# A two-layer transformer kernel with routed experts: the last steps of attention 1 reordered, its last query loads issued one per step

## The reference

```
x = x + tanh(g_xattn[1]) * attention_1(layernorm(x), ctx)      # per block: 32 heads of 8, causal, 128 x 128
z = layernorm(x)                                               # per token
logits = z @ w_gate                                            # [2048, 8]
idx = argmax(softmax(logits))                                  # one of E = 8 experts for a token
loc = cumsum(onehot(idx)) - onehot(idx)                        # place in that expert's queue
keep = loc < 256                                               # capacity: 2048 / 8
h = gelu(dispatched(z) @ w1[e]);  y = h @ w2[e]                # per expert, 256 tokens, 256 -> 1024 -> 256
x = x + tanh(g_ffn[1]) * gate * y                              # back to the kept tokens
```

## Time and profile before

| | |
|---|---|
| median of 3 runs | 1349.39 us (1348.5 to 1352.16) |
| the profiled execution's own time | 1351.38 us |
| its span, first to last instruction | 1349.6 us |
| busy: TensorE, VectorE, ScalarE, POOL | 1253.2, 1092.6, 946.8, 705.6 us |
| chain that ended last | TensorE 77%, VectorE 14%, unexplained issue 3%, ScalarE 2%, DMA 2%, POOL 1% |
| TensorE's granted clock, mean | 0.98 of full speed |

### The profile page before, as it was taken

How to read it: one execution, slowest core, us unless ns; L and a number is a source line. 1 busy time by engine, 2 the same in 40 slices (tenths; PEclk the granted TensorE clock), 3 DMA queues, 4 the chain that set the end, 5 groups by cost and what they waited for, 6 DMA issues and landing times.

```text
span 1349.6 us, 28140 instructions
## 1 busy us (share of the span) xinstructions
PE 1253.2 (93%) x10492; PEld 1091.1 (81%) x10492; DVE 1092.6 (81%) x2203; ACT 946.8 (70%) x2153; POOL 705.6 (52%) x618
## 2 busy tenths in 40 slices
PE   1688999999999999999999999979999999995998
PEld 1577999999999999999999999866776454454998
DVE  8979889999989999989999999986434778765554
ACT  5799877778887778887788887645122466572775
POOL 5657555565665566655655554442000356563575
PEclk9889999999999999999999999999999999996999
DMA  4222332222123222133221010024544324217662
GB/s 146 87 62 69 99 95 87 76 71 65 54 78 88 76 69 68 52 79 89 65 70 35 26 36 24 23 68 140 64 75 72 67 42 74 60 45 242 214 231 80
DMA packets 117574, 110.05 MB, mean 82 GB/s; under 512 B 12187, under 2 KB 101499, under 8 KB 117312
## 3 DMA queue, kind: packets, MB, share of 16 engines
q1 hardware_dynamic: 114320, 99.03, 27.5%
q0 software_dynamic: 2944, 9.19, 1.9%
q10 hardware_dynamic: 176, 0.04, 0.0%
HBM read 80.20 MB, written 28.07 MB: 80 GB/s over the span
## 4 chain that ended last, share of the span: by engine, by line
PE 77%; DVE 14%; issue 3%; ACT 2%; DMA 2%; POOL 1%; POOLq 0%; SPq 0%; ACTq 0%; DVEq 0%
PE PC L577 8%; PE SS L543 7%; PE PO L559 7%; PE B L521 5%; PE PA L479 4%; PE PA L481 4%; PE B L1224 3%; PE PO L1208 2%; PE B L1734 2%; PE SS L535 2%; PE PA L492 2%; PE PA L491 2%; PE PA L493 2%; PE SS L2276 2%; PE PA L504 2%
## 5 line engine op out<-in xcount | busy, mean ns | idle before, releaser
L1021 POOL TENSOR_TENSOR RB<-YS,M 128x512 bf16<-128x512 f32 x128 | 161.3, 1260 | 279.4 <-DVE YS L860 279.4
L665 ACT ACTIVATE QT<-B,sm 128x256 f32<-128x256 f32 x256 | 131.3, 566 | 142.2 <-PE B L521 141.7
L479 PE MATMUL PA<-WH,XQ 128*128 128x256 f32 x512 | 141.0, 307 | 17.9 <-DVE WL L808 13.3
L1016 POOL TENSOR_TENSOR yy<-vv,half 128x14 f32<-128x14 f32 (+1 forms) x64 | 147.6, 2306 | 5.3
L543 PE MATMUL SS<-QT,KT 128*128 128x256 f32 x512 | 133.1, 382 | 7.8 <-DVE mx L812 7.6
L481 PE MATMUL PA<-WL,XQ 128*128 128x256 f32 x512 | 130.1, 286 | 0.0
L824 DVE TENSOR_REDUCE vv<-SQ 128x7 f32<-128x896 f32 (+1 forms) x128 | 120.7, 943 | 0.3 <-ACT SQ L711 0.3
L479 PEld LDWEIGHTS PA<-WH,XQ 128*128 128x128 f32 x512 | 98.9, 193 | 19.1 <-DVE WL L808 13.7
L832 DVE TENSOR_TENSOR QN<-QN,yy 128x512 f32<-128x512 f32 x128 | 114.0, 891 | 0.0
L812 DVE TENSOR_REDUCE mx<-SS 128x4 bf16<-128x512 f32 x128 | 88.0, 687 | 26.2 <-PE SS L535 25.2
L521 PE MATMUL B<-identf,QN 128*128 128x128 f32 x768 | 105.7, 274 | 2.0 <-ACT LNT L620 1.1
(11 more groups left out here) (359 smaller groups left out, 4120.6 us busy)
## 6 DMA issues: line engine op xcount, KB each, us to landing
W<-in_w SPq DMA_DIRECT2D x16, 1024.0 KB
XK<-xk_d SPq DMA_DIRECT2D x24, 512.0 KB, 4.3
V<-v_d SPq DMA_DIRECT2D x112, 64.0 KB
v_d<-VST SPq DMA_DIRECT2D x48, 128.0 KB, 2.0
Q<-qsc SPq DMA_DIRECT2D x48, 128.0 KB
WR<-in_wprojT SPq DMA_DIRECT2D x16, 256.0 KB, 3.0
xk_d<-XK SPq DMA_DIRECT2D x8, 512.0 KB, 3.9
kt_d<-KT SPq DMA_DIRECT2D x64, 64.0 KB, 1.6
```

The source lines that it names most:

```text
L479: pe.matmul(PA[:, 256 * k:256 * k + 256], XQ[:, k, c, bs], wh[:, c, 256 * k:256 * k + 256], start=c == 0, stop=False)
L665: a.activation(QT[i % 2][:, o:o + 256], B1[:, o:o + 256], ACT.Identity, bias=col(n + "b"), scale=col(n + "w"))
L1016: p.tensor_tensor(yy[j % 2][:, :, 0:n], v_, half[:, 0:2 * n].rearrange("p (h k) -> p h k", h=2), ALU.pow).then_inc(s_rstd, 1)
L1021: p.tensor_tensor(RB[i % 2][:], YS[:], M[:], ALU.subtract).then_inc(s_rb, 1)
```

## The change

Five things are altered, all in the order of calls, banks and waits.

1. SyncE: the last quad's twelve loads are issued one a step, steps 33 to 44 (`sp_last_queries`), each after a wait on the count of products (`sp_pace`). The row writes of blocks 0 to 7 begin at step 45 and have the same wait. Those of blocks 8 to 11 follow two a step from step 66, in place of one group after the loop; those of 12 to 15 are written block by block. The weights of expert 1 are issued when the first gather has landed.
2. Blocks 8 to 11 are scaled in steps 65 to 68, turned in steps 66 to 69 and have their logits in steps 68 to 71; blocks 12 and 13 are scaled and turned in the loop too, each with a root of its own. The loop has one step less. Logits of blocks 8 to 15 lie in bank `B2`, eight columns each, and are copied four blocks at once.
3. The last two turns, u = 30 and 31, go to the two halves of `PO` and wait for the last exponential, not for another block's copy or residual.
4. The first choice is made in step 72, before the normalisations 30 and 31. It compares the logits with their maximum directly, and the subtraction moves behind the one-hot.
5. The places lie in `POa` instead of `B2`, the products of `who` and `whose` in one bank, `B1`; VectorE reads both halves of `who` in one operation where it had two.

```diff
-        TR = [SS, PC]
+        TR = [SS[:], PC[:]]
-        next_bs = [range(0, 4), range(4, 8), range(8, 12), range(12, 15), range(15, 16)]
-        NEXT = {32: 0, 48: 1, 64: 2}
-        LAST = N1 + 11
+        next_bs = [range(0, 4), range(4, 8), range(8, 12), range(12, 13), range(13, 14), range(14, 15), range(15, 16)]
+        NEXT = {32: 0, 48: 1, 63: 2, 67: 3, 71: 4}
+        LAST = N1 + 10
...
+        def logits_at(b):
+            return PC[:, 256:256 + E] if b < 8 else B2[:, E * (b - 8):E * (b - 7)]
+        def turn_bank(u):
+            return {2 * NB - 2: POa, 2 * NB - 1: POb}.get(u, TR[u % 2])
...
+        def sp_pace(sp, n):
+            sp.wait_ge(*((s_S, N + n) if n <= N1 else (s_ST, N + n - 8)))
+        def sp_last_queries(sp, i):
...
+            sp.dma_start(Q6[r0:r0 + 8, 3, :, :], src[:, :, 1536:2048]).then_inc(s_qg[3], 16)
...
-                    if b in (2, 3, 7, 8):
-                        sp_queries(sp, 2 + b // 7, b in (3, 8))
+                    if b in (2, 3):
+                        sp_queries(sp, 2, b - 2)
+                if 33 <= n < 45:
+                    sp_pace(sp, n)
+                    sp_last_queries(sp, n - 33)
...
         def pe_turn_1(pe, u):
-            if u % 2 == 0 and b:
+            if b == NB - 1:
+                pe.wait_ge(s_ex, N + N1)
+            elif b and u % 2 == 0:
                 pe.wait_ge(s_oe, b)
-            if u % 2 and b:
+            elif b:
                 pe.wait_ge(s_add, N + b)
...
+                if n == 73:
+                    pe_next_turn(pe, 13)
+                if n == 72:
+                    pe_turn_1(pe, 30)
...
-            pe_logits(pe, 11)
             pe_turn_1(pe, 31)
+            pe_out_proj(pe, 14)
+            pe_logits(pe, 12)
+            pe_out_turn(pe, 15)
+            pe_logits(pe, 13)
             pe_queue_places(pe, 0)
-            pe_out_turn(pe, 15)
             pe_out_proj(pe, 15)
-            for b in (12, 13, 14):
+            for b in (14, 15):
                 pe_next_turn(pe, b)
-            for b in (12, 13, 14):
                 pe_logits(pe, b)
...
+                if n == 72:
+                    dve_next_scale(v, 4, next_bs[4])
+                    dve_logits_quad(v, 2)
+                    dve_choose(v, 0)
+                if n == 73:
+                    dve_normalise(v, 30)
+            dve_normalise(v, 31)
             dve_residual_1(v, 14)
...
         def sp_experts(sp):
             after_attention_1(sp)
+            sp.wait_ge(s_d[0], 32)
...
         def dve_choose(v, k):
             v.tensor_reduce(mx, lg, AX, ALU.max).then_inc(*vs.up())
-            v.tensor_tensor(lg, lg, bc(mx, n), ALU.subtract).then_inc(s_sub, 1)
-            v.tensor_scalar(oh, lg, 0.0, None, ALU.is_equal).then_inc(*vs.up())
+            v.tensor_tensor(oh, lg, bc(mx, n), ALU.is_equal).then_inc(*vs.up())
...
-            v.tensor_tensor(one, oh, bc(mx, n), ALU.is_equal).then_inc(s_oh, 1)
+            v.tensor_tensor(one, oh, bc(first, n), ALU.is_equal).then_inc(s_oh, 1)
+            v.tensor_tensor(lg, lg, bc(mx, n), ALU.subtract).then_inc(s_sub, 1)
```

More of the change, by code:

```diff
@@ L1650, in sp_queries @@
                     s_qg[q4], 16)
+        def sp_pace(sp, n):
+            sp.wait_ge(*((s_S, N + n) if n <= N1 else (s_ST, N + n - 8)))
+        def sp_last_queries(sp, i):
+            half, z = divmod(i, NP)
+            if i == 0:
+                sp.wait_ge(s_qst[3], 32)
+            src = qsc[QPART[z]].rearrange("(a h d) t -> h d a t", h=2, d=8)[half]
+            r0 = 64 * half + 8 * z
+            sp.dma_start(Q6[r0:r0 + 8, 3, :, :], src[:, :, 1536:2048]).then_inc(s_qg[3], 16)
         def sp_attention_1(sp):
@@ L1669, in sp_attention_1 @@
                 for k in range(2):
-                    if 0 <= n - 12 * k - 42 < 12:
-                        sp_next_row(sp, 4 * k + (n - 12 * k - 42) // 3, (n - 12 * k - 42) % 3)
+                    if 0 <= n - 12 * k - 45 < 12:
+                        sp_pace(sp, n)
+                        sp_next_row(sp, 4 * k + (n - 12 * k - 45) // 3, (n - 12 * k - 45) % 3)
+                for p in range(2 * (n - 66), 2 * (n - 66) + 2):
+                    if 0 <= p < 12:
+                        sp_next_row(sp, 8 + p // 3, p % 3)
             sp_load_w(sp, 0)
-            for k in range(2, 5):
-                sp_next_rows(sp, k)
+            for b in range(12, NB):
+                for part in range(3):
+                    sp_next_row(sp, b, part)
         def pe_raw(pe, i):
@@ L1788, in pe_logits @@
             pe.wait_ge(s_xt, b + 1)
+            if b >= 12:
+                pe.wait_ge(s_lg, 12)
             for c in range(2):
-                t = pe.matmul(next_bank(b)[:, 256:256 + E], XF[:, c, 128 * b:128 * b + 128], WG[:, c, :], start=c == 0, stop=c == 1)
+                t = pe.matmul(logits_at(b), XF[:, c, 128 * b:128 * b + 128], WG[:, c, :], start=c == 0, stop=c == 1)
             t.then_inc(s_lgp, 1)
@@ L1834, in pe_attention_1 @@
                     pe_next_turn(pe, b)
-                u = every(n, 2, 13, 2 * NB)
+                u = every(n, 2, 13, 2 * NB - 2)
                 if u is not None:
@@ L1938, in act_attention_1 @@
                     act_last_queries_middle(a, (n - 24) // 4)
+            act_next_turn(a, 13)
             act_out_turn(a, 15)
-            for b in (12, 13, 14):
-                act_next_turn(a, b)
+            act_next_turn(a, 14)
+            act_next_turn(a, 15)
             act_split_w1(a, 0, 0)
-            act_next_turn(a, 15)
         def dve_maximum_1(v, i):
@@ L2023, in dve_attention_1 @@
             for n in range(8, LAST):
-                u = every(n, 2, 14, 2 * NB)
+                u = every(n, 2, 14, 2 * NB - 2)
                 if u is not None:
@@ L2160, in build @@
         OHB = R[:, :, 2, :]
-        locs = B2[:, 0:128]
+        locs = POa[:, 0:128]
         SETS = (range(0, 12), range(12, NB))
-        who = (B1[:, 0:3 * E], PC[:, 0:3 * E])
-        whose = (B1[:, 3 * E:6 * E], PC[:, 3 * E:6 * E])
+        who = (B1[:, 0:3 * E], B1[:, 3 * E:6 * E])
+        whose = (B1[:, 6 * E:9 * E], B1[:, 9 * E:12 * E])
+        who_kez = B1[:, 0:6 * E].rearrange("p (z k e) -> p k e z", z=2, k=3)
         s_slots, s_sub, s_exp, s_oh, s_A, s_who, s_idx, s_wgt, s_hi, s_whose = (
@@ L2249, in pe_weights @@
                     t = pe.matmul(whose[z], A[:, b, 128 * z:128 * z + 128], RW[:, b].rearrange("p k e -> p (k e)"),
-                                  start=b == 0, stop=b == NB - 1)
+                                  start=b + z == 0, stop=b + z == NB)
             t.then_inc(s_whose, 1)
@@ L2428, in dve_routing @@
             v.wait_ge(s_who, 3)
-            for z in range(2):
-                w = who[z]
-                v.tensor_copy(TU[:, :, z], w[:, E:2 * E]).then_inc(*vs.up())
-                v.wait_ge(*vs.at())
-                v.scalar_tensor_tensor(out=TI[:, :, z], in0=w[:, 0:E], scalar=128.0, in1=TU[:, :, z], op0=ALU.mult,
-                                       op1=ALU.add).then_inc(*vs.up())
+            v.tensor_copy(TU[:], who_kez[:, 1]).then_inc(*vs.up())
+            v.wait_ge(*vs.at())
+            v.scalar_tensor_tensor(out=TI[:], in0=who_kez[:, 0], scalar=128.0, in1=TU[:], op0=ALU.mult, op1=ALU.add).then_inc(
+                *vs.up())
             v.wait_ge(*vs.at())
```

97 lines of the change are left out of this document (45 added, 52 removed).

## The result

The changed kernel takes **1345.97 us** in the median of 13 runs (1341.14 to 1349.90); the kernel before, run beside it, 1350.44 (1347.41 to 1360.87). The ratio is 0.9949 with a 95% interval from 0.9931 to 0.9967: faster by 0.5%, some 6.9 us (4.5 to 9.3). The two medians lie only 4.5 us apart and the averages 6.8, since the kernel before has some longer runs, up to 1360.87. The profiled execution took 1345.7 us, its span 1344.0.

A forecast was written before the change was run, and what follows sets the result against it. TensorE was taken to bound the kernel, with losses from late maxima in attention 1's loop and a serial, low-clock tail. Terms -3.9 + 1.5 - 5.75 - 0.4 - 1.0 = -9.55 us took 1349.39 to 1339.8, range 1337 to 1345.

The forecast's parts named there:

- Loads, -3.9: Attention 1's loop: last quad's query loads, one per step, no longer delay the maxima TensorE waits for; 3.9 us less.
- Turns inside the loop, +1.5: Before the last score product: TensorE's added turns and logits of blocks 8 to 11 cost 2.2 us, gaps hide 0.7.
- To the last logits, -5.75: From last score product to last logits: 14.4 us instead of 20.15, with TensorE's high clock until block 15's output projection.
- Choice and indices, -0.4: From last logits to the gather's indices: one choice operation and one copy-and-combine pair fewer, 0.4 us less.
- Weights, -1.0: Expert 0's gather: with expert 1's weights held back until it lands, it takes 1.0 us less than 5.25.
- The rivals: Four alternatives: tail keeps its length (chance 0.12), maxima still late (0.07), kernel slower (0.04), expert 1's weights late (0.06).
- The maxima are on time at block 10: Rival in attention 1's loop: slower single loads make block 10's maxima late, loop gains nothing, 1343.7 us; chance 0.07.
- the two tail terms: Rival after the last score product: turns inside the loop and shorter tail, together -4.25 us, become 0; 1344.1 us, chance 0.12.
- the standstill: VectorE, after the last score product, waits about 1 us for POOL's root before block 13's scaling, with logits 8 to 11 ready.
- ScalarE did not wait for expert 1's weights: Rival at the experts: expert 1's weights arrive 15 us after the gather, costing 3 us, 1342.9 us; chance 0.06.

The follow-up runs named there:

- the third profile: The changed kernel, unaltered, timed again beside the second run with its query loads back in two batches; ratio to the kernel before 0.9955, median 1345.13 us.
- the tail alone: The changed kernel with the last quad's query loads in two batches again; against the kernel before 0.9944, when run again 0.9987 (median 1349.05 us).

## Why the prediction was right or wrong

*Loads, -3.9:* right. The steps ahead of the first products of blocks 8 and 9 are 1.26 and 2.63 us shorter, 3.89 in all; the rest of what differs to block 14 are two single steps near the start that vary between executions (block 3's maxima 0 to 1.2 us late, one step 1.3 us longer in the third profile).

*Turns inside the loop, +1.5:* +1.39 in each profile. One part was not in the list, the 0.57 us behind the new root's input; so the gaps hid some 1.4 of 2.8 us, not 0.7 of 2.2. That the total fits is in part luck: the two misses cancel.

*To the last logits, -5.75:* -5.56, and the steps one by one: 3.67 to the copy behind scaling 13 (3.7), 2.05 for copy and choice (2.1), 1.18 for two normalisations (1.3), 1.43 for TensorE (1.6), 1.44 for the projection (1.3), 1.34 for residual to guess (1.45), 0.67 for the root (0.7), 2.81 for the rest (2.0 and 0.25). Only the last was mis-sized: not one turn but also the logits behind it ran at the low clock, 1.02 us for 0.51.

*Choice and indices, -0.4:* -0.44.

*Weights, -1.0:* wrong, in the step "Without company I take nearly the lowest". The range of landing times was read as the effect of company; but with the weights beside it and no fetch the gather needed 3.89 us to the tokens' turn, without them and with the fetch 5.32. The change leaves the fetch about where it was (2.6 us after the second issue before, 2.0 now), so the term is 0, one end of its bounds.

*The time.* 1339.8 was 6.2 us too low, and 1345.97 is outside the range. Of this, 1.0 us is the failed term. The sum without it, -8.55, lies 0.1 us beyond the best of the three profiles (-6.8 to -8.4) and inside the measured 4.5 to 9.3; -9.55 lies just outside. A further 1.05 us is the base: the kernel before had a median of 1349.39 in the three runs I counted from and 1350.44 beside the changed one; beside the experiments it had 1354.61, 1353.60 and 1350.05. The other 4.1 us belong to no term: 1.7 are the step from 8.55 to the 6.9 of the ratio, well inside its interval, and 2.4 that from the 6.9 to the 4.5 between the medians. Against 1349.39 the ratio gives 1342.5 (1340.1 to 1344.9). The range took in each term's bounds and nearly nothing of the base's own spread.

*The rivals* did not come. The maxima are on time at block 10; the two tail terms did not vanish, though the standstill was there; ScalarE did not wait for expert 1's weights (first product of expert 1 13.75 us after the first of expert 0, 13.59 before; the copy of its weights follows ScalarE's own work without a wait).

## What to carry to other kernels

Small transfers that an engine waits for should not stand behind a batch of large ones in one queue; spread the batch to the consumer's step, and its price can be read beforehand from the spacing of the small ones. Order a tail by its chain, row by row from the trace: it came out within 0.2 us of 14.6, but taking out one stand gave only half, as the next engine's order then held the rest. Before a transfer's spread is explained by other traffic, list when code is fetched, and give the base's own spread a place in the range.

## What the runs showed of the hardware

One 16.4 KB fetch of TensorE's instructions, falling 2.0 to 2.6 us behind the second issue of a gather of two times 256 KB, went with a gather 0.8 to 1.9 us longer (4.65 to 5.45 us against 3.55 to 3.89 in the fourteen profiles), and the first expert waited for it. Moved ahead of the issue in the same kernel, it left 3.57 us where the changed kernel has 4.80 to 5.45. The Trainium skill has the fetch in blocks of 16 KiB, of a cost that is "mostly hidden" (Runtime: NRT & Kernel Launch, Instruction fetch mechanics): the size agrees, and here a cost was not hidden, that on the gather. That one of the 16 engines carries the fetch and its share of the gather is argued from the single late packets; what the shift of the fetch did is shown, in one profile, and the other thirteen agree.

A wait of 2.36 us was followed by about 3 us at 1.2 GHz in both profiles of the tail alone, and a wait of 2.46 us by none in the kernel before. From block 4 on the score steps of all profiles agree within 0.1 us wherever neither late maxima nor an edit moves them. The first of them starts anywhere from 1063.82 to 1070.15, so some 6 us of spread between executions come from ahead of it.
